# Four finish buffers, row scatters ahead of result scatters, and a new order of the router on three engines

## What is computed

```python
x = x + conv_block(layernorm_over_channels(x))      # two quantised 3x3 convolutions
t = tokens(x)                                       # 16384 x 64
r = layernorm(t)
probs = softmax(r @ router_w.T)                     # 8 experts
top_p, top_i = top_k(probs, 2); gates = top_p / (sum(top_p) + 1e-9)
y = sum over the two chosen e: gate_e * ((silu(r @ w1[e].T) * (r @ w3[e].T)) @ w2[e].T)   # hidden 682
out = t + y
```

## Time and profile before

| | |
|---|---|
| median of 3 runs | 960.22 us (957.41 to 960.74) |
| the profiled execution, its own time | 957.29 us |
| its span, first to last instruction | 955.5 us |
| TensorE matmul busy | 800.2 us, 84% |
| VectorE busy | 612.8 us, 64% |
| ScalarE busy | 429.6 us, 45% |
| POOL busy | 486.3 us, 51% |
| TensorE's mean granted clock | 0.92 of full speed |

### The profile page before, as it was taken

The page is one execution under the profiler, slowest core; times in us unless marked ns, Lnnn a source line. Parts: engine busy times, 40 slices in busy tenths (PEclk is TensorE's granted clock), DMA queues, the critical chain, the costliest instruction groups (busy, mean ns, idle before and its releaser), DMA issues.

```text
span 955.5 us, 20465 instructions
## 1 busy us (share of the span) xinstructions
PE 800.2 (84%) x6017; PEld 568.2 (59%) x6017; DVE 612.8 (64%) x1891; ACT 429.6 (45%) x911; POOL 486.3 (51%) x393
## 2 busy tenths in 40 slices
PE   9989877875898968999999999989586869668493
PEld 6734465653566746677767777756454646446372
DVE  4977668787486867677677777656453636446362
ACT  6435345543244433455546666545243534234141
POOL 3510067777067774367743333535333636456456
PEclk9989979977999999999999999999797979879797
DMA  8940011211465647577766776756554657547352
GB/s 273 236 71 1 22 67 47 70 50 49 163 177 132 179 93 224 143 210 219 200 171 165 184 181 167 195 146 146 138 144 111 148 117 187 128 93 188 71 127 14
DMA packets 119946, 130.10 MB, mean 136 GB/s; under 512 B 40972, under 2 KB 94104, under 8 KB 119872
## 3 DMA queue, kind: packets, MB, share of 16 engines
q1 hardware_dynamic: 83968, 110.24, 37.3%
q0 software_dynamic: 35904, 19.03, 15.6%
HBM read 97.80 MB, written 29.01 MB: 133 GB/s over the span
## 4 chain that ended last, share of the span: by engine, by line
PE 34%; DMA 7%; issue 5%; DVE 5%; POOL 4%; SPq 3%; ACT 1%; POOLq 0%; DVEq 0%; ACTq 0%
PE bank L1626 21%; PE bank L1641 10%; DMA out<-finish_sum,finish_rows 4%; POOL out L621 2%; POOL out L632 2%; DMA rest_results<-gated 2%; PE bank L1608 2%; DVE conv_all L1336 1%; DMA conv_all<-pair_rows 1%; PE bank L1600 1%; SPq L478 1%; SPq L479 1%; SPq L493 1%; DVE gated L1360 0%; ACT xT L813 0%
## 5 line engine op out<-in xcount | busy, mean ns | idle before, releaser
L1626 PE MATMUL bank<-xT,w 64*128 64x256 f32 x1496 | 268.3, 408 | 93.5 <-DVE conv_all L1336 92.9
L799 ACT ACTIVATE conv_all<-bank 128x512 f32<-128x512 f32 x340 | 203.0, 597 | 238.8 <-PE bank L1626 238.0
L1336 DVE TENSOR_TENSOR conv_all<-conv_all,bank 128x512 f32<-128x512 f32 x340 | 229.1, 686 | 118.5 <-ACT conv_all L799 116.9
L1626 PE MATMUL bank<-xT,w_second 64*128 64x256 f32 x1496 | 245.4, 392 | 0.0
L1626 PEld LDWEIGHTS bank<-xT,w 64*128 64x128 f32 x1496 | 153.0, 195 | 150.7 <-DVE conv_all L1336 103.7
L621 POOL DMA_INDIRECT out<-conv_all,dest_all x72 | 113.4, 1575 | 135.8 <-DVE conv_all L1363 103.8
L590 POOL DMA_INDIRECT pair_rows<-y_and_rows,slot_all x128 | 126.2, 986 | 108.5 <-issue 103.1
L1626 PEld LDWEIGHTS bank<-xT,w_second 64*128 64x128 f32 x1496 | 165.1, 197 | 17.9
L1641 PE MATMUL bank<-conv_all,w 128*64 128x256 f32 x680 | 161.8, 385 | 2.4 <-DVE tile_map L1170 2.4
L1641 PE MATMUL bank<-conv_all,w_second 128*64 128x256 f32 x680 | 161.8, 385 | 0.0
L1641 PEld LDWEIGHTS bank<-conv_all,w 128*64 128x64 f32 x680 | 87.8, 137 | 53.2 <-issue 14.5
(11 more groups left out here) (275 smaller groups left out, 1071.3 us busy)
## 6 DMA issues: line engine op xcount, KB each, us to landing
w<-in_w SPq DMA_DIRECT2D x68, 384.0 KB
w_second<-in_w SPq DMA_DIRECT2D x68, 384.0 KB
w<-in_w2t SPq DMA_DIRECT2D x68, 192.0 KB
w_second<-in_w2t SPq DMA_DIRECT2D x68, 192.0 KB
conv_all<-pair_rows SPq DMA_DIRECT2D x96, 68.0 KB, 1.9
x_all<-in_x SPq DMA_DIRECT2D x8, 512.0 KB, 4.1
x_all<-y_and_rows POOLq DMA_DIRECT2D x16, 256.0 KB, 7.0
out<-x_all SPq DMA_DIRECT2D x8, 512.0 KB, 2.8
```

Of the source, the lines that this page charges most:

```text
L799: nc.scalar.activation(sbuf[k % 3], h1_ps[k % 3][:], ACT.Silu).then_inc(silu_rdy, 1)
L1336: V.tensor_tensor(hbuf[k], sbuf[k % 3], h3_ps[k % 3][:], ALU.mult).then_inc(mul_rdy, 1)
L1626: ins = mm(ps[k % 3][:, TH * of:TH * of + TH], wbuf[of][u][half, cols], xT[u][half, tokens], start=True, stop=True)
```

## The change

In words, part by part:

- Finish steps have four sets of buffers (`FR = 4`) in place of two; all waits on `fin_rdy` and `fin_out` reach back four steps. POOL takes the finish steps of tile j + 1 right behind result j (before: those of tile j). The padding region of the output grows from six to eight blocks of 256 rows.
- POOL scatters all 128 row groups before the first result, and the padding behind result 8 in place of 10.
- In router steps 1 to 7 ScalarE takes the exponentials ahead of its copies of raw rows.
- TensorE issues constants in the router: 16 ahead of `positions` in step 0, 7 ahead of `turn_rows` in steps 1 to 6, 26 at the end of step 6. Each run first waits until the copy of the bank that it writes is done (`raw_kept`), except the last, which writes a convolution's bank.
- VectorE's pieces between tiles are cut up and moved: `place` over tiles 3 and 4, `pad_places` to 5, `read_map` and `turn_map` from 5 to 6, `segment_starts` without its copies in 9 (the copies, `list_places`, in 10), `block_rows` in 11, `late_places` in 13 and its `place` over 14 and 15, `unit_experts` in 17, `unit_rows` in 18; their last three instructions (`late_map`) stay in 24.

```diff
+    FR = 4
-    PADS = 6 * TH
+    PADS = 8 * TH
...
-        fin_in = [sb(f"finish_in{u}", [128, 2, 2, YROW])[:, :, :, :] for u in range(2)]
-        fin_sum = [sb(f"finish_sum{u}", [128, 2, C])[:, :, :] for u in range(2)]
+        fin_in = [sb(f"finish_in{u}", [128, 2, 2, YROW])[:, :, :, :] for u in range(FR)]
+        fin_sum = [sb(f"finish_sum{u}", [128, 2, C])[:, :, :] for u in range(FR)]
...
-                    if n >= 2:
-                        sp.wait_ge(fin_rdy, n - 1)
+                    if n >= FR:
+                        sp.wait_ge(fin_rdy, n - FR + 1)
                     else:
                         sp.wait_ge(dummy_out, 48)
                     sp.wait_ge(gated_out, 16 * (stored - G0))
...
-                u = n % 2
+                u = n % FR
                 wait_apart(pool, fin_rdy, n + 1)
-                if n >= 2:
-                    wait_apart(pool, fin_out[u], 32 * (n // 2))
+                if n >= FR:
+                    wait_apart(pool, fin_out[u], 32 * (n // FR))
...
-            for j in range(NT + 1):
-                while rows_done < min(88 + int(4.5 * j), GH * NS):
+            for j in range(NT):
+                while rows_done < GH * NS:
                     scatter_row(rows_done)
                     rows_done += 1
                 if j == 0:
                     wait_apart(pool, raw_out, 16 * NP)
                     wait_apart(pool, dummy_out, 48)
-                if j < NT:
-                    scatter_y(j, j % 4)
-                if j == 10:
+                scatter_y(j, j % 4)
+                if j == 8:
                     scatter_pads()
...
-                for _ in FINISH.get(j, ()):
+                for _ in FINISH.get(j + 1, ()):
                     finish(fins_done)
...
                 if first:
                     exps(p)
+                if not first:
+                    exps(p)
                 if last != 1:
                     keep_raw(p + 1)
-                if not first:
-                    exps(p)
...
-                    dve.wait_ge(fin_rows[u], 16 * (n - u) + 32)
-                    if n >= 2:
-                        dve.wait_ge(fin_out[u], 32 * (n // 2))
+                    dve.wait_ge(fin_rows[u], 32 * (n // FR) + 32)
+                    if n >= FR:
+                        dve.wait_ge(fin_out[u], 32 * (n // FR))
...
                 if j == 3:
-                    place(2, tile_no[:, 0:1])
+                    place(2, tile_no[:, 0:1], 1)
+                if j == 4:
+                    place(2, tile_no[:, 0:1], 2)
+                if j == 5:
+                    pad_places()
                 if j == 6:
-                    pad_places()
                     rests()
...
                 if j == 10:
+                    list_places()
+                if j == 11:
                     block_rows()
-                if j == 12:
+                if j == 13:
                     late_places()
+                if j == 14:
+                    place(2, slot_state[:, 2:3], 1)
+                if j == 15:
+                    place(2, slot_state[:, 2:3], 2)
+                if j == 17:
+                    unit_experts()
+                if j == 18:
+                    unit_rows()
                 if j == G0 - 4:
-                    unit_experts()
-                    unit_rows()
+                    late_map()
...
                 if first:
+                    pe.wait_ge(raw_kept, 4)
+                    keep_busy(16, raw_ps[1])
                     positions(p)
+                elif last != 1:
+                    pe.wait_ge(raw_kept, 2 * p + 4)
+                    keep_busy(7, raw_ps[1])
                 if last != 1:
                     turn_rows(p + 1)
...
                 if not last:
                     conv_pair(p + 2)
+                if last == 2:
+                    keep_busy(26, conv_ps[0])
```

More of the change, by code:

```diff
@@ L290, in conv_moe_kernel @@
         gated_out = sem("gated_out")
-        fin_rows = [sem(f"finish_rows_in{u}") for u in range(2)]
+        fin_rows = [sem(f"finish_rows_in{u}") for u in range(FR)]
         fin_rdy = sem("finish_ready")
-        fin_out = [sem(f"finish_out{u}") for u in range(2)]
+        fin_out = [sem(f"finish_out{u}") for u in range(FR)]
         rT_rdy = sem("rows_turned")
@@ L527, in _ @@
                 sp.wait_ge(y_out[v], 32 * (NT // 4))
-            for u in range(2):
-                sp.wait_ge(fin_out[u], 32 * (NG // 2))
+            for u in range(FR):
+                sp.wait_ge(fin_out[u], 32 * (NG // FR))
         @block.gpsimd
@@ L1136, in less_before, with place @@
                 one(V.tensor_tensor(out_, of, run[:, at, Z:Z + n], ALU.subtract))
-            def place(levels, number):
+            def place(levels, number, part=0):
                 n = slice(0, NG * levels)
                 a_, in_t = a[:, n], in_[:, n]
+                if part == 2:
+                    place_prefs(levels)
+                    return
                 one(V.tensor_scalar(a_, less[:, n], number, None, ALU.add))
@@ L1150, in place, with place_prefs @@
                 one(V.tensor_reduce(tcol[:, 0:1], a_, AX.X, ALU.add))
+                if part == 0:
+                    place_prefs(levels)
+            def place_prefs(levels):
+                n = slice(0, NG * levels)
                 for i in range(2):
@@ L1273, in unit_experts @@
                 one(V.tensor_tensor(unit_pref, unit_pref, unit_rest, ALU.mult))
-                late = prefs[:, :, G0:G1]
-                one(V.tensor_tensor(late, late, unit_pref.rearrange("p (s i) -> p i s", i=2), ALU.add))
-                V.tensor_scalar(tmap[:, 1:3, G0:G1], prefs[0:1, :, G0:G1], -128.0, 128.0 * E, ALU.mult, ALU.add)
             def unit_rows():
@@ L1285, in unit_rows, with late_map @@
                 one(V.tensor_tensor(unit_at, unit_at, unit_rest, ALU.mult))
+            def late_map():
+                late = prefs[:, :, G0:G1]
+                one(V.tensor_tensor(late, late, unit_pref.rearrange("p (s i) -> p i s", i=2), ALU.add))
+                V.tensor_scalar(tmap[:, 1:3, G0:G1], prefs[0:1, :, G0:G1], -128.0, 128.0 * E, ALU.mult, ALU.add)
                 of_slot = slot_rows[0:1, G0:G1].unsqueeze(2).broadcast_to([1, NU // 2, 2])
@@ L1418, in tile @@
                     hidden(j, k)
-                if j == 5:
+                if j == 6:
                     read_map(y_ps[:, TH:TH + 3 * SL], 2, FULL[0], G0)
@@ L1653, in tile @@
                 ins.then_inc(xt_rdy, 1)
-                if isinstance(j, int) and j in (5, G0 - 4):
-                    turn_map(2 if j == 5 else 3, y_ps[:, TH:TH + 3 * SL])
-                    pe.wait_ge(tmap_rdy, 2 if j == 5 else 3)
+                if isinstance(j, int) and j in (6, G0 - 4):
+                    turn_map(2 if j == 6 else 3, y_ps[:, TH:TH + 3 * SL])
+                    pe.wait_ge(tmap_rdy, 2 if j == 6 else 3)
                 for k in range(0, KT, 2):
@@ L1704, in layouts @@
     table[:, 428], table[:, 429] = 2 * p, 2 * p + 1
-    for v in range(6):
+    for v in range(8):
         for q in range(2):
```

20 lines of the change are left out of this document (10 added, 10 removed).

## The result

The changed kernel takes 859.69 us (median of four runs, 858.66 to 860.52), the kernel before 959.4 us (four runs): a ratio of 0.8962, with a 95% interval of 0.894 to 0.8983. The forecast was 856. The profiled execution took 860.52 us with a span of 858.8 us, 96.7 us less than the span of before.

What follows compares the result with a forecast made beforehand. Matmuls set the pace, 8.25 us a tile, with late tiles slowed by waits A and B and VectorE's chain bounding the router. Savings of 74 + 3.7 + 9.7 + 7 + 10 = 104 us gave 856 us for a median, range 844 to 870.

Steps and rivals of the forecast that it cites:

- Finish stretch: The 29 tiles from 590 to 932 us: four finish buffers were to save 74 us net, bounds 53 and 84.
- rows and pieces: Ahead of the finish stretch: sending all row groups first saves 9.7 us, cutting VectorE's planning pieces saves 7 us.
- end: POOL's last result comes 3.7 us earlier, a finish step then standing ahead of result 66; bounds 0 and 3.7.
- router: Router steps: exponentials first on ScalarE and constants on TensorE save 10 us, bounds 3 and 12.5.
- Wait A: Finish tiles: SP stands at a store just issued, delaying the row loads behind it; 26 us, expected to stay.
- wait B: Finish tiles: VectorE's finish step waits for scatters of the step two before; 77 us, expected to go with four buffers.
- the rival of the half clock: Router: clock stays half, as a rule on transposes implies; 3 us saved in place of 10, 863 us; chance 0.07.
- SP's queue as the next limit: Finish tiles without wait A: rows land later, 1 to 1.5 us lost each, 873 to 881 us; chance 0.13.
- POOL's scatters: Rival at the end: 2.1 us a scatter in place of 1.86 makes POOL the bound, 866 us; chance 0.04.
- the rival of full DMA engines: Last 30 tiles: DMA load over 1.0 makes weights late, slower than before at 960 to 970 us; chance 0.02.

## Why the prediction was right, and which of its steps was not

**The sum held.** 104 us were forecast, 96.7 came in the profiled pair. Finish stretch 74 against 70.9, rows and pieces 16.7 against 15.4, end 3.7 against 3.8, router 10 against 6.6. Wait A stayed, with the five waits that were named.

**The step that failed is the cause given for wait B**: "With four buffers a step waits for the one four back ... So wait B goes." The size and the place were right, the reason only in part: four buffers do it in the old order (864.0), but POOL's order alone does it with two. The prediction worked out 11 to 15 us from step to landing and set that only against the 25 us of four buffers, not against what two give. Its 11 to 15 were too long as well: with two buffers and the new order the one wait left ended 8.9 us after the step that it waited for (802.06 to 810.99). It counted the new order only at the end, 3.7 us, and did not ask what it does to the landing in each tile, though the earlier trace rows say it: the scatters began late because in POOL's order they stood behind one more result.

**The router** repeats it on a small scale. "Moving the exponentials removes VectorE's 9.8 us" is true only where the constants don't: with constants and late exponentials 1.2 us of it are left. The size was near: 6.6 in the profiled execution, 9.3 with late exponentials and 10.6 in the run with two buffers, whose router is the same as the change's (below). The clock of the router, windows from 116 to 217 us, was 0.85 before, and in the changed kernel:

```profile
116.00:217.00 101.00, 85.46 (x569) 57.83 (x567) 81.16 (x251) 53.36 (x108) 71.78 (x72) 0.98 0.18 61
```

So the rival of the half clock did not come. The turns of raw rows, by line, before and after (duration in ns: least, median, greatest):

```profile
L1541 PE MATMUL bank<-ident,x x64: 272/273/422, 105.9 to 216.0; 128*128 128x128 f32 x64
```

```profile
L1566 PE MATMUL bank<-ident,x x64: 272/273/273, 106.4 to 209.2; 128*128 128x128 f32 x64
```

All 64 ran at one pace, none stretched to 422. The rule of the Trainium skill, "TensorE: Matmul & The Clock Gate", Part 4 (PE-mode transpose), that the full clock does not engage for transposes, costs nothing here, eight to a step between other matmuls; whether a long run of them would, no run here shows.

**The parts do not add up one by one.** Undone alone, the buffers cost nothing, the order 4.3, the rows 16.6, the pieces 6.8, constants 2.4, exponentials nothing: 30 us of 100. Undone in the groups that share a wait, 75.2 + 16.6 + 6.8 + 6.9 = 105.5, somewhat more than the whole, 99.7. The rows cost more beside faster tiles than the 9.7 for which they were priced: gaps of 10.13 and 5.46 us for 7.20 and about 1. But the intervals of the two largest terms, 5 us either way each, are as wide as the difference, so that it may be noise.

**The rivals.** SP's queue as the next limit did not show in tiles with one step. It came with two steps a tile: in tiles 57 and 62 of the changed kernel, where the prediction had taken off 1 to 2 us each and VectorE waited 2.2 and 1.1 us, and in all six as soon as wait A was gone, where it cost 1 to 2.4 us. That is near the 1 to 1.5 of the rival, though by issue time; late landing came only with the loads ahead of the weights. Wait A, priced at 26 us, gave 16.5 when every step was due one tile later, since the finish loads behind it came to light. POOL's scatters kept to 1.56 us. The DMA share in the finish stretch is 0.73, so the rival of full DMA engines is out as well.

## What to carry to other kernels

Ask of a wait for a buffer not only how many buffers there are, but what stands ahead of the release in the releasing engine's own queue; moving that by one item may do what twice the memory does. Where a change has two edits that could each end a wait, price each alone and both together: undoing one shows nothing if the other suffices. A wait that is taken away uncovers the next one behind it, here SP's issue time, and a wait for data grows when the work ahead of it gets faster.

## What was not expected of the hardware

The same router instructions reached the first tile at 242.58 us in the changed kernel's profile and at 238.59 in that of the run with two buffers. VectorE's last step of the router, and windows from 116 to 130 us with the granted clock, each first of the changed kernel, then of that run:

```profile
224.93 0.65 DVE L1087 TENSOR_TENSOR positions<-bank,base 128x476 f32<-128x476 f32 x1 [1.21 <-PE bank L1586]
```

```profile
221.26 0.65 DVE L1087 TENSOR_TENSOR positions<-bank,base 128x476 f32<-128x476 f32 x1 [0.80 <-PE bank L1586]
```

```profile
116.00:130.00 14.00, 10.73 (x72) 8.51 (x70) 7.66 (x19) 4.29 (x7) 6.13 (x7) 0.88 0.14 50
```

```profile
116.00:130.00 14.00, 10.68 (x76) 7.58 (x75) 8.68 (x26) 7.21 (x13) 7.38 (x8) 1.00 0.16 55
```

Of the 4.0 us, 1.5 are there at L1087 in step 0 (118.70 against 117.15), and 1.3 come in step 1, where the clock was 0.88 in the one and 1.00 in the other. Steps 2 to 7 add 0.8, and all that follows 0.3. From 224 to 231 us, where TensorE runs constants, the two clocks were 0.78 and 1.00, but that cost little: in both traces TensorE then stood waiting for VectorE's plan of the tiles, 2.14 and 3.31 us. What decides at which of the two levels (1.2 and 2.4 GHz) a stretch runs was not tried. The first tile's time so carries up to 4 us that no edit explains, and this is why differences of 2 us between these runs are not read as effects of an edit.

SP's time to issue was the other surprise: four finish loads take 3.66 us or more of its queue wherever they stand, some 0.92 us each. The Trainium skill, "DMA: Bandwidth & Descriptors", Issuing engines are not separate DMA queues, calls the sequencer's time for a DMA "usually small relative to the DMA itself". Here the trace disagrees: 0.92 us stand beside 1.9 us from issue to landing, the median of these loads in the run that has them ahead of the weights. Where four of them go out just ahead of the rows, they make the tile longer.
